# A transformer block on one Trainium2 core: the adapter's scores and softmax made beside the q projection, its products with the values from one compact 40-row tile

## The chip, the cores and the metric

The kernel runs on one core of a Trainium2 chip, as one program in one launch. Its time is the device time of one execution in microseconds (us); lower is better. The engines are PE (TensorE: matmuls, with PEld for its weight loads), DVE (VectorE), ACT (ScalarE), POOL (GpSimd) and SP (SyncE), which here only issues DMAs. PE writes to PSUM, eight banks of 128 x 512 f32; POOL neither reads nor writes it.

## The reference, cut to what matters

The attention of the block adds to the ordinary causal output, head by head, a second softmax over ten adapter tokens. Its scores use the rotated q of the same head, its scale is that of the whole width (C = 1024), and it has no mask:

```python
q = _apply_rope(q, cos, sin)                       # T = 2048, 32 heads of 32
...
_, ak, av = jnp.split(jnp.einsum('btc,oc->bto', adapter_wte[None], w_attn), 3, axis=-1)   # 10 tokens
ascores = jnp.einsum('bhqd,xhkd->bhqk', q, ak) / jnp.sqrt(jnp.asarray(C, x.dtype))
ascores = gating[0] * jax.nn.softmax(ascores, axis=-1)
y = y + jnp.einsum('bhqk,xhkd->bhqd', ascores, av)
```

Around it stand a modulated layernorm and the qkv projection (in front of it), and the output projection and a mixture of eight experts, two for each token (behind it).

## The kernel before

The program has three stages, and a barrier of all engines stands between them: `front`, `attention` and `tail`.

**front.** The normalized input lies in SBUF as hT_hi and hT_lo, two f32r parts of an f32 number, and each product is three matmuls (hi x hi, hi x lo, lo x hi). The loop over `n` makes 64 units, 32 of k and then 32 of q. A unit is one weight tile (128 columns, a group of four heads) times a quarter of the tokens (512): 8 steps k of 3 matmuls (L602 to L604) into one of two PSUM banks `acc[:, n % 2]`. Units go in halves of 16: four quarters times four weight tiles. DVE then rotates the unit (`rotate`: L406, L407, L409, L410) into `y[:, n % 2]`, ACT rounds it to y_hi (L264), POOL takes the rest y_lo in the place of y (`low_y`, L482), and SP stores both (`store`, L175). `rotate(n)` waits until the stores of unit n - 2 have landed. Between units PE also does parts of the modulation (`mod`, L523, from a 2 MB weight load into w_raw) and of the adapter's keys and values; POOL splits the next half's weights (L470, L472, L487). The 32 tiles of v (L625, L632) follow. The adapter's keys `ak` and values `av` end as tiles of 128 x 128 for each group of four heads, zero outside the four 32 x 32 blocks of a head with itself; in each block ten columns of ak, and ten rows of av, are used.

**attention.** Before its main loop stands a head of 16 turns (`TURNS`). A turn is one group of four heads times 1024 tokens: SP loads q_hi and q_lo (`load_pair`, L862, 512 KB each), POOL adds them (`a_add`, L1346), PE makes the scores with eight f32 matmuls of 40 columns (`a_score`, L1043), DVE takes the largest, subtracts, sums and inverts (L1290, L1294, L1299, L1301), ACT takes the exponential (L1152), POOL multiplies into `a_prob`, ten of every 32 columns (`a_spread`, L1353), PE transposes eight times (`a_turn_over`, L1053), ACT copies (L1158), PE multiplies av by it twice, 512 columns each and both in the one bank `y_acc` (`a_multiply`, L1062), ACT copies (L1164) and stores (L1169) to `scratch_a_y`, from where the main loop reads it back.

Spread over the turns by `head_share`, PE and DVE do the first 76 of the items with which the main loop later finds each row's largest score (`see`, L976 on PE, three banks `seen`; `largest`, L1237 or L1243 on DVE), which need the quarters of q and k that SP loads (`load_quarter`, L846). An item of PE waits until DVE has freed its bank. The main loop starts with L999, after a pair of L1095.

## Time and profile before

| | us |
|---|---|
| three timed runs | 2723.43, 2725.85, 2728.96 |
| their median | 2725.85 |
| profiled execution | 2727.61 |
| its span from the first instruction to the last | 2725.7 |
| its mean granted TensorE clock | 0.947 of full speed |

The profiled execution is 1.9 us longer than its span; what lies around the span is launch and end. It is 1.8 us longer than the median. In a row of a timeline stand the start, the time from the first to the last of what it merges, the engine and the line; behind it, in square brackets, the idle time before it with what ended it. Rows 2 are of the 32 units of q and of the head of the attention stage.

### The profile page before, as it was taken

The numbers are of one execution on the slowest core, as the hardware profiler recorded it, in microseconds if no ns is written. First come the engines' busy times: TensorE is split into PE (matmuls) and PEld (weight loads), VectorE is DVE, ScalarE is ACT, GpSimd is POOL, SyncE is SP. The second block draws the span as 40 slices with busy tenths as digits, with TensorE's granted clock in tenths as the row PEclk, the third lists the DMA queues.
The fourth block names the chain that finished last, engine by engine and source line by source line (L and its number), as shares of the span: only waits on it lengthen the run. The fifth ranks groups of instructions, "written<-read, shape, count | busy, mean of one in ns | idle before, by whom it ended". The sixth has DMA issues, their size and how long they took to land. (4 is left out here: it accounts for less than half of the span.)

```text
span 2725.7 us, 39161 instructions
## 1 busy us (share of the span) xinstructions
PE 2491.5 (91%) x13391; PEld 1630.1 (60%) x13391; DVE 1593.0 (58%) x3130; ACT 1051.3 (39%) x1860; POOL 1313.7 (48%) x824
## 2 busy tenths in 40 slices
PE   6789999999578999999999999998889876999997
PEld 4667676777454444444444444443368765888885
DVE  5544554210256777777777777777236554777665
ACT  3420011111135655555555555555601111444443
POOL 4351442100365766676766676765724452332332
PEclk8899999999589999999999999998989887999998
DMA  7356556311953524252515151513266745888885
GB/s 265 109 155 201 160 165 183 100 39 51 223 202 103 113 55 111 56 115 54 116 49 120 42 131 40 133 34 79 77 203 216 168 113 183 305 299 294 302 287 178
DMA packets 224849, 397.18 MB, mean 146 GB/s; under 512 B 43756, under 2 KB 94380, under 8 KB 224564
## 3 DMA queue, kind: packets, MB, share of 16 engines
q1 hardware_dynamic: 199588, 319.56, 40.9%
q0 software_dynamic: 17152, 50.38, 5.3%
q10 hardware_dynamic: 7952, 25.21, 2.9%
q8 instruction: 91, 1.49, 0.2%
q14 instruction: 66, 0.54, 0.1%
HBM read 299.16 MB, written 103.76 MB: 148 GB/s over the span
## 5 line engine op out<-in xcount | busy, mean ns | idle before, releaser
L1397 POOL TENSOR_TENSOR t_two<-t_prob 128x1024 f32<-128x1024 f32 (+1 forms) x321 | 688.2, 2164 | 181.1 <-ACT t_prob L1207 107.7
L1207 ACT ACTIVATE t_prob<-t_scores_psum 128x512 f32<-128x512 f32 (+3 forms) x1280 | 611.1, 537 | 387.8 <-PE t_scores_psum L999 194.9
L1237 DVE TENSOR_REDUCE t_part<-t_seen_psum 128x1 f32<-128x512 f32 x768 | 480.8, 681 | 165.3 <-PE t_seen_psum L976 161.0
L976 PE MATMUL t_seen_psum<-t_k_stack,t_q_stack 96*128 96x512 f32 (+3 forms) x1283 | 517.1, 412 | 24.2 <-DVE t_part L1237 15.8
L999 PE MATMUL t_scores_psum<-t_q_stack,t_k_stack 97*128 97x512 f32 (+3 forms) x1280 | 506.1, 407 | 5.9 <-ACT t_prob L1207 4.4
L999 PEld LDWEIGHTS t_scores_psum<-t_q_stack,t_k_stack 97*128 97x128 f32 x1280 | 244.0, 191 | 310.0 <-ACT t_prob L1207 172.4
L1243 DVE CUSTOM_DVE_ANT_0 t_seen_psum<-t_seen_psum,t_causal 128x128 f32<-128x128 f32 (+3 forms) x515 | 250.0, 504 | 106.3 <-PE t_seen_psum L976 96.1
L1019 PE MATMUL t_y_acc_psum<-t_prob,t_v 128*32 128x512 f32 (+3 forms) x2560 | 304.9, 549 | 0.0
L976 PEld LDWEIGHTS t_seen_psum<-t_k_stack,t_q_stack 96*128 96x128 f32 x1283 | 253.2, 199 | 67.1 <-DVE t_part L1237 30.7
L1678 PE MATMUL acc_psum<-z_e_hi,z_x_hi 128*128 128x512 f32 x576 | 228.3, 396 | 0.0
L1680 PE MATMUL acc_psum<-z_e_hi,z_x_lo 128*128 128x512 f32 x576 | 225.2, 391 | 0.0
L1679 PE MATMUL acc_psum<-z_e_lo,z_x_hi 128*128 128x512 f32 x576 | 224.7, 390 | 0.0
L602 PE MATMUL f_acc_psum<-hT_hi,f_w_hi 128*128 128x512 f32 x512 | 208.4, 407 | 2.0 <-POOL f_w_lo L472 1.7
L603 PE MATMUL f_acc_psum<-hT_lo,f_w_hi 128*128 128x512 f32 x512 | 202.8, 396 | 0.0
L604 PE MATMUL f_acc_psum<-hT_hi,f_w_lo 128*128 128x512 f32 x512 | 202.3, 395 | 0.0
L482 POOL TENSOR_TENSOR f_y<-f_y,f_y_hi 128x512 fp32r<-128x512 f32 x64 | 83.8, 1310 | 219.9 <-ACT f_y_hi L264 219.5
L264 ACT ACTIVATE f_y_hi<-f_y 128x512 fp32r<-128x512 f32 x64 | 40.4, 631 | 333.8 <-DVEq L411 333.7
L1032 PE MATMUL t_total_psum<-t_two,t_ones 128*32 128x512 f32 (+1 forms) x1296 | 160.7, 569 | 1.9 <-POOL t_two L1397 1.9
L1748 ACT ACTIVATE z_x_hi<-z_turned_psum 128x1024 fp32r<-128x1024 f32 x38 | 38.7, 1019 | 223.6 <-PE z_turned_psum L1664 223.6
L602 PEld LDWEIGHTS f_acc_psum<-hT_hi,f_w_hi 128*128 128x128 f32 x512 | 98.3, 192 | 40.4 <-issue 9.1
L1680 PEld LDWEIGHTS acc_psum<-z_e_hi,z_x_lo 128*128 128x128 f32 x576 | 108.5, 188 | 23.0
L1679 PEld LDWEIGHTS acc_psum<-z_e_lo,z_x_hi 128*128 128x128 f32 x576 | 108.7, 189 | 21.6
(240 smaller groups left out, 3804.1 us busy)
## 6 DMA issues: line engine op xcount, KB each, us to landing
z_raw<-in_expert_w SPq DMA_DIRECT2D x80, 512.0 KB, 5.3
z_spare<-in_expert_w SPq DMA_DIRECT2D x72, 512.0 KB
f_w_raw<-in_wmod SPq DMA_DIRECT2D x8, 2048.0 KB, 10.1
t_q_stack<-scratch_q_hi SPq DMA_DIRECT2D x64, 256.0 KB, 5.3
t_k_stack<-scratch_k_hi SPq DMA_DIRECT2D x64, 256.0 KB, 5.2
f_w_raw<-in_w_attn SPq DMA_DIRECT2D x24, 512.0 KB, 6.1
t_inverse<-scratch_inverse SPq DMA_DIRECT2D x132, 64.0 KB
t_y<-scratch_a_y SPq DMA_DIRECT2D x33, 256.0 KB
```

What stands on the lines that cost most here:

```text
L602: nc.tensor.matmul(acc[:, n % 2], lhs[0], rhs[0], start=(k == 0), stop=False)
L603: nc.tensor.matmul(acc[:, n % 2], lhs[0], rhs[1], start=False, stop=False)
L976: nc.tensor.matmul(seen[:, n % BANKS, 0:width], q_stack[par][0:STACK, h, t0:t0 + P], k_stack[par][0:STACK, h, c * CH:c * CH + width], star ...
L999: last = nc.tensor.matmul(scores[:, score_bank(step, h), c0:CH], k_stack[par][0:TOPS, h, kt * P:(kt + 1) * P], q_stack[par][0:TOPS, h, qc ...
L1019: last = nc.tensor.matmul(y_acc[h * D:(h + 1) * D, c0:CH], v[par][:, kt, h * D:(h + 1) * D], prob[:, step % RING, h, c0:CH], start=(kt == ...
L1207: nc.scalar.activation(prob[:, step % RING, h, c0:CH], scores[:, score_bank(step, h), c0:CH], ACT.Exp, scale=1.0 / math.sqrt(D)).then_inc( ...
L1237: nc.vector.tensor_reduce(dst, seen[:, n % BANKS], AX.X, ALU.max).then_inc(seen_free, 1)
L1243: nc.vector.tensor_tensor_reduce(out=at, in0=at, in1=causal[:, CH - width:CH], scale=1.0, scalar=MASKED, op0=ALU.add, op1=ALU.max, accum_o ...
L1397: nc.gpsimd.tensor_tensor(two[:, pair % 2, heads, c0:CH], a, b, ALU.add).then_inc(two_ready, 1)
L1678: nc.tensor.matmul(acc[:, s, col], x_hi[:, s, k], e_hi[:, k, col], start=(k == 0), stop=False)
L1679: nc.tensor.matmul(acc[:, s, col], x_hi[:, s, k], e_lo[:, k, col], start=False, stop=False)
L1680: last = nc.tensor.matmul(acc[:, s, col], x_lo[:, s, k], e_hi[:, k, col], start=False, stop=(k == KC - 1))
```

## The change

Scores and softmax leave the attention stage and are made in `front`, unit by unit, straight from the f32 tile `y[:, n % 2]` of a unit of q (`ask`, four matmuls; `lower`, `exponent`, `invert`, `spread`). They land in the PSUM banks `turned`, and in the second half of the tile av, which is not yet written then, and in the tile stats. The names `av`, `f_stats` and `f_turned` in the order's rows are these. SP stores 160 probabilities for each of 128 tokens of each unit to a new scratch in HBM (`store_prob`). The attention stage loads them with four DMAs (`load_prob`), and no q. Its 16 turns become 32 (`ASKS`) of 512 tokens: four transposes of 40 columns into 40 x 512, one ACT copy, and one matmul with `a_v`, a tile of 40 rows (ten for each head) that four DMAs gather from av into the tile `both`. Its product goes in turn to a bank of `scores` and to `y_acc`. POOL has in the head only the gating product and the memsets left. The items of `see` are the same, spread over the 32 turns on PE and in one row on DVE.

```diff
+        AM = TPC * HG
+        spare = av[:, G // 2:G, :].rearrange("p g n -> p (g n)")
+        weight = spare[:, 0:2 * AM * A].rearrange("p (b m a) -> p b m a", b=2, a=A)
+        prob = spare[:, 2 * AM * A:3 * AM * A].rearrange("p (m a) -> p m a", a=A)
...
+            def store_prob(m):
+                _, i, q, s = place(QUERIES + m)
+                t, x = (i * HG + s) * (NQ // 2) + q // 2, q % 2
+                sp.wait_ge(prob_ready, m + 1)
+                sp.dma_start(a_prob_d[t, :, x * AM * A:(x + 1) * AM * A], prob.rearrange("p m a -> p (m a)")).then_inc(prob_stored, 16)
...
+                if asked(n) >= 3:
+                    store_prob(asked(n) - 3)
...
+            def exponent(m):
+                act.wait_ge(shifted, m + 1)
+                at = weight[:, m % 2].rearrange("p m a -> p (m a)")
+                nc.scalar.activation(at, at, ACT.Exp, scale=1.0 / math.sqrt(C)).then_inc(exp_done, 1)
...
+            def lower(m):
+
+                dve.wait_ge(scored, m + 1)
+                if m > 0:
+                    dve.wait_ge(shifted, m)
+                view = turned[:, m % 2, 0:AM * A].rearrange("p (m a) -> p m a", a=A)
+                nc.vector.tensor_reduce(top, view, AX.X, ALU.max).then_inc(topped, 1)
+                dve.wait_ge(topped, m + 1)
+                if m >= 2:
+                    dve.wait_ge(prob_ready, m - 1)
+                nc.vector.tensor_tensor(weight[:, m % 2], view, top.rearrange("p (m a) -> p m a", a=1).broadcast_to([P, AM, A]),
+                                        ALU.subtract).then_inc(shifted, 1)
+
+            def invert(m):
+                dve.wait_ge(exp_done, m + 1)
+                if m > 0:
+                    dve.wait_ge(inv_ready, m)
+                nc.vector.tensor_reduce(total, weight[:, m % 2], AX.X, ALU.add).then_inc(summed, 1)
+                dve.wait_ge(summed, m + 1)
+                if m >= 1:
+                    dve.wait_ge(prob_ready, m)
+                nc.vector.reciprocal(inv, total).then_inc(inv_ready, 1)
...
+                if asked(n) >= 2:
+                    invert(asked(n) - 2)
+                if asked(n) >= 1:
+                    lower(asked(n) - 1)
+            invert(QUERIES - 2)
+            lower(QUERIES - 1)
+            invert(QUERIES - 1)
...
+                if asked(n) >= 0:
+                    pool.wait_ge(scored, asked(n) + 1)
...
+            def spread(m):
+                pool.wait_ge(inv_ready, m + 1)
+                if m >= 1:
+                    pool.wait_ge(prob_stored, 16 * m)
+                nc.gpsimd.tensor_tensor(prob, weight[:, m % 2], inv.rearrange("p (m a) -> p m a", a=1).broadcast_to([P, AM, A]),
+                                        ALU.mult).then_inc(prob_ready, 1)
...
+            def ask(m):
+
+                _, i, q, s = place(QUERIES + m)
+                n = QUERIES + m
+                pe.wait_ge(y_ready, n + 1)
+                if m == 0:
+                    pe.wait_ge(hi_done, NQ * KC)
+                    pe.wait_ge(second_taken, number_of["adapter_k", 1] - FIRST_EVENTS + 1)
+                if m >= 2:
+                    pe.wait_ge(shifted, m - 1)
+                for j in range(TPC):
+                    last = nc.tensor.matmul(turned[:, m % 2, j * HG * A:(j + 1) * HG * A], y[:, n % 2, j * P:(j + 1) * P],
+                                            ak[:, i * HG + s].rearrange("p (h a) -> p h a", a=D)[:, :, 0:A], start=True, stop=True)
+                last.then_inc(scored, 1)
...
+                    if k == ASK_AT and asked(n) >= 1:
+                        ask(asked(n) - 1)
...
+        a_v = both[0:HG * A].rearrange("p b n -> p (b n)").rearrange("p (g n) -> p g n", n=P)
+        a_turned_at = lambda u: scores[0:HG * A, u % 2]
+        a_acc = lambda u: scores[:, 2] if u % 2 == 0 else y_acc[:, :]
...
+            def load_prob(b):
+                at = slice(b * TURNS // 4, (b + 1) * TURNS // 4)
+                sp.dma_start(a_prob[:, at], a_prob_d[at].rearrange("t p n -> p t n")).then_inc(a_prob_loaded[b], 16)
+
+            sp.dma_start(ident[:, :], consts["ident"]).then_inc(consts_loaded, 16)
+            load_prob(0)
+            for h in range(HG):
+                sp.dma_start(a_v[h * A:(h + 1) * A, :, :], av[h * D:h * D + A, :, :]).then_inc(a_v_loaded, 16)
+            sp.dma_start(gating[:, :], consts["gating"].rearrange("(a n) -> a n", a=1).broadcast_to([P, 1])).then_inc(a_v_loaded, 16)
...
+            for dst, name in ((causal[:, :], "causal"), (after, "after")):
+                sp.dma_start(dst, consts[name]).then_inc(consts_loaded, 16)
...
+            def a_turn_over(u):
+
+                t, x = divmod(u, 2)
+                if t % (TURNS // 4) == 0:
+                    pe.wait_ge(a_prob_loaded[t // (TURNS // 4)], 16)
+                if u >= 2:
+                    pe.wait_ge(a_turn_ready, u - 1)
+                for j in range(TPC):
+                    cols = slice((x * TPC + j) * HG * A, (x * TPC + j + 1) * HG * A)
+                    last = nc.tensor.transpose(a_turned_at(u)[:, j * P:(j + 1) * P], a_prob[:, t, cols], ident[:, :])
...
+            pe.wait_ge(consts_loaded, 48)
+            for u in range(ASKS + 1):
+                if u < ASKS:
+                    a_turn_over(u)
+                head(u, 0)
+                if u >= 1:
+                    a_multiply(u - 1)
+                head(u, 1)
...
+            for n in range(HEAD):
+                advance(0, n)
...
+            pool.wait_ge(a_v_loaded, 80)
+            nc.gpsimd.tensor_scalar(a_v[:, :, :], a_v[:, :, :], gating[0:HG * A, 0:1], None, ALU.mult).then_inc(a_gated, 1)
+            pool.wait_ge(a_gated, 1)
+            for b in range(2):
                 nc.gpsimd.memset(k_stack[b][STACK:TOPS, :, :].bitcast(F32), 1.0).then_inc(one_rows_set, 1)
...
+                nc.tensor.matmul(a_acc(u), a_v[:, u // NQ], a_turn[:, u % 2], start=True, stop=True).then_inc(a_acc_ready, 1)
```

`asked(n)` is n - 32. `ask(asked(n) - 1)` stands inside unit n, after its step k = 5, and takes the tile of unit n - 1. On PE, in the front, this is a place inside a unit of q, before:

```order
L602 MATMUL f_acc_psum<-hT_hi,f_w_hi 128x512
L603 MATMUL f_acc_psum<-hT_lo,f_w_hi 128x512
L604 MATMUL f_acc_psum<-hT_hi,f_w_lo 128x512
L602 MATMUL f_acc_psum<-hT_hi,f_w_hi 128x512
L603 MATMUL f_acc_psum<-hT_lo,f_w_hi 128x512
```

and of the change:

```order
L697 MATMUL f_acc_psum<-hT_lo,f_w_hi 128x512
L698 MATMUL f_acc_psum<-hT_hi,f_w_lo 128x512
L680 MATMUL f_turned_psum<-ak,f_y 128x40 x4
L696 MATMUL f_acc_psum<-hT_hi,f_w_hi 128x512
L697 MATMUL f_acc_psum<-hT_lo,f_w_hi 128x512
```

The four matmuls of 40 columns stand among the 24 of the unit, with six of its matmuls behind them; nothing else of the unit moved. On PE, in the head of attention, one turn before (t_seen is an item's bank):

```order
L1053 MATMUL t_scores_psum<-t_ident,a_prob 128x128 x8
L1043 MATMUL t_scores_psum<-ak,a_q 128x40 x8
L976 MATMUL t_seen_psum<-t_k_stack,t_q_stack 128x384
L976 MATMUL t_seen_psum<-t_k_stack,t_q_stack 128x512
L1062 MATMUL t_y_acc_psum<-a_turn,av 128x512 x2
L976 MATMUL t_seen_psum<-t_k_stack,t_q_stack 128x128
L976 MATMUL t_seen_psum<-t_k_stack,t_q_stack 128x256
L1053 MATMUL t_scores_psum<-t_ident,a_prob 128x128 x8
L1043 MATMUL t_total_psum<-ak,a_q 128x40 x8
```

and two turns of the change:

```order
L1073 MATMUL t_seen_psum<-t_k_stack,t_q_stack 128x512 x2
L1142 MATMUL t_scores_psum<-t_ident,a_prob 40x128 x4
L1073 MATMUL t_seen_psum<-t_k_stack,t_q_stack 128x512
L1151 MATMUL t_scores_psum<-a_turn,t_both 128x512
L1073 MATMUL t_seen_psum<-t_k_stack,t_q_stack 128x512
L1142 MATMUL t_scores_psum<-t_ident,a_prob 40x128 x4
L1080 MATMUL t_seen_psum<-t_ident,t_top 16x128
L1151 MATMUL t_y_acc_psum<-a_turn,t_both 128x512
L1073 MATMUL t_seen_psum<-t_k_stack,t_q_stack 128x512
L1142 MATMUL t_scores_psum<-t_ident,a_prob 40x128 x4
```

The scores' matmuls (40 columns) are gone from here, the two products stand in different banks, and the items stand in smaller groups between them. On SP, at the start of the attention stage, before:

```order
L862 DMA a_q_hi<-scratch_q_hi 128x1024
L862 DMA a_q_lo<-scratch_q_lo 128x1024
L846 DMA t_q_stack<-scratch_q_hi 32x4x512
L846 DMA t_q_stack<-scratch_q_lo 32x4x512
L846 DMA t_q_stack<-scratch_q_hi 32x4x512
L846 DMA t_k_stack<-scratch_k_hi 32x4x512 x2
L846 DMA t_k_stack<-scratch_k_lo 32x4x512
L872 DMA t_ident<-in_ident 128x128
L872 DMA t_causal<-in_causal 128x512
L872 DMA t_y_own<-in_after 128x128
L872 DMA t_gating<-in_gating 128x1
L862 DMA a_q_hi<-scratch_q_hi 128x1024
```

and of the change (t_both is the tile of values):

```order
L957 DMA t_ident<-in_ident 128x128
L955 DMA a_prob<-scratch_a_prob 128x4x320
L960 DMA t_both<-av 10x1024 x4
L961 DMA t_gating<-in_gating 128x1
L938 DMA t_q_stack<-scratch_q_hi 32x4x512
L938 DMA t_q_stack<-scratch_q_lo 32x4x512
L938 DMA t_q_stack<-scratch_q_hi 32x4x512
L938 DMA t_k_stack<-scratch_k_hi 32x4x512 x2
L938 DMA t_k_stack<-scratch_k_lo 32x4x512
L964 DMA t_causal<-in_causal 128x512
L964 DMA t_y_own<-in_after 128x128
L938 DMA t_q_stack<-scratch_q_hi 32x4x512
```

The pair of q is gone; one load of probabilities, and four small ones inside SBUF, stand ahead of the first quarter of q and k.

## Rows read from the trace of the kernel before

**Rows 1.** The page: the span, and the busy time of each engine

```profile
span 2725.7 us, 39161 instructions
...
PE 2491.5 (91%) x13391; PEld 1630.1 (60%) x13391; DVE 1593.0 (58%) x3130; ACT 1051.3 (39%) x1860; POOL 1313.7 (48%) x824
```

**Rows 2.** Windows: length; busy PE, PEld, DVE, ACT, POOL; clock; DMA share; GB/s

```profile
285.70:490.10 204.40, 191.24 (x836) 142.64 (x834) 105.47 (x168) 24.26 (x36) 69.49 (x46) 0.97 0.58 170
...
682.50:851.20 168.70, 118.30 (x543) 82.97 (x543) 70.78 (x179) 43.52 (x65) 78.80 (x39) 0.77 0.68 195
```

**Rows 3.** Timeline, the start of the attention stage

```profile
682.53 0.35 SPq L862 DMA_DIRECT2D a_q_hi<-scratch_q_hi  x1
...
699.18 0.23 DVE L1230 CAST t_ident_b<-t_ident 128x128 bf16<-128x128 f32 x1 [15.84 <-DMA t_gating<-in_gating]
```

**Rows 4.** Groups of instructions, window 682.5 to 851.2

```profile
L1346 POOL TENSOR_TENSOR a_q<-a_q_hi,a_q_lo 128x1024 f32<-128x1024 f32 x16 | 37.6, 2350 | 154.4 <-DMA a_q_lo<-scratch_q_lo 154.4
...
L1237 DVE TENSOR_REDUCE t_part<-t_seen_psum 128x1 f32<-128x512 f32 x44 | 28.0, 682 | 9.2 <-PE t_seen_psum L976 8.9
...
L1164 ACT ACTIVATE a_y<-t_y_acc_psum 128x512 f32<-128x512 f32 x32 | 19.0, 593 | 31.5 <-PE t_y_acc_psum L1062 31.5
...
L1158 ACT ACTIVATE a_turn<-t_scores_psum 128x1024 f32<-128x1024 f32 x16 | 16.4, 1024 | 19.6 <-PE t_scores_psum L1053 19.6
...
L1243 DVE CUSTOM_DVE_ANT_0 t_seen_psum<-t_seen_psum,t_causal 128x128 f32<-128x128 f32 (+3 forms) x32 | 15.0, 510 | 6.6 <-PE t_seen_psum L976 6.6
...
L1353 POOL TENSOR_TENSOR a_prob<-a_weight,a_inv 128x320 f32<-128x320 f32 x16 | 11.8, 737 | 25.7 <-DVE a_inv L1301 25.6
...
L1299 DVE TENSOR_REDUCE a_total<-a_weight 128x32 f32<-128x320 f32 x16 | 7.6, 476 | 0.0
```

**Rows 5.** Timeline of PE, late turns of the head

```profile
809.65 3.63 PE L1043 MATMUL t_scores_psum<-ak,a_q 128*128 128x40 f32 x16 [5.31 <-POOL a_q L1346]
...
816.77 1.10 PE L1062 MATMUL t_y_acc_psum<-a_turn,av 128*128 128x512 f32 x2 [0.78 <-ACT a_y L1164]
...
819.28 1.88 PE L1043 MATMUL t_total_psum<-ak,a_q 128*128 128x40 f32 x16
820.99 0.71 PE L976 MATMUL t_seen_psum<-t_k_stack,t_q_stack 96*128 96x512 f32 x2
821.54 1.02 PE L1062 MATMUL t_y_acc_psum<-a_turn,av 128*128 128x512 f32 x2
823.42 1.10 PE L1062 MATMUL t_y_acc_psum<-a_turn,av 128*128 128x512 f32 x2 [0.86 <-ACT a_y L1164]
823.95 1.26 PE L976 MATMUL t_seen_psum<-t_k_stack,t_q_stack 96*128 96x512 f32 x3
...
827.62 0.70 PE L976 MATMUL t_seen_psum<-t_k_stack,t_q_stack 96*128 96x512 f32 x2
...
847.54 1.10 PE L1062 MATMUL t_y_acc_psum<-a_turn,av 128*128 128x512 f32 x2 [0.78 <-ACT a_y L1164]
...
851.18 0.50 PE L999 MATMUL t_scores_psum<-t_q_stack,t_k_stack 97*128 97x512 f32 x1
```

**Rows 6.** Timeline, one ordinary unit of q, from 450.65

```profile
450.65 0.39 PE L602 MATMUL f_acc_psum<-hT_hi,f_w_hi 128*128 128x512 f32 x1
...
453.17 0.69 DVE L410 TENSOR_TENSOR f_y<-f_y,f_x_rot 128x512 f32<-128x512 f32 x1
...
456.09 0.39 PE L602 MATMUL f_acc_psum<-hT_hi,f_w_hi 128*128 128x512 f32 x1
```

**Rows 7.** Timeline of PE, start of a half's modulation work

```profile
308.85 3.64 PE L523 MATMUL f_small_psum<-f_w_raw,f_silu_rep 128*32 128x512 f32 x16 [5.31 <-DMA f_w_raw<-in_wmod]
```

**Rows 8.** Timeline, a rotation beside a weight split of POOL

```profile
474.16 2.39 POOL L487 TENSOR_TENSOR f_w_lo<-f_w_raw,f_w_hi 128x1024 fp32r<-128x1024 f32 x1 [1.89 <-ACT f_w_hi L271]
...
474.29 2.81 DVE L409 TENSOR_TENSOR f_x_rot<-f_x_rot,f_cos_sin 128x512 f32<-128x512 f32 x1 [0.15 <-DVE f_y L407]
```

**Rows 9.** DMA issues: KB each, median us from issue to landing

```profile
scratch_v<-f_y_hi SPq DMA_DIRECT2D x32, 256.0 KB, 2.3
```

More of the change, by code:

```diff
@@ L220, in _ @@
                         load_w(5, slot)
+                if 1 <= m <= 3:
+                    store_prob(QUERIES - 4 + m)
                 store_v(m)
@@ L507, in _ @@
                 low_y(n)
+                if asked(n) >= 3:
+                    spread(asked(n) - 3)
                 if u > HALF_UNITS - HG and half < 3:
@@ L511, in _ @@
                     split_w((half + 2) * HG - 1)
+            for m in range(QUERIES - 3, QUERIES):
+                spread(m)
             even_w(5 * HG, 4 * HG + 3)
@@ L647, in _ @@
                         lead(m + 1)
+                    else:
+                        ask(QUERIES - 1)
                     pe.wait_ge(w_ready, 4 * HG + 2 * hv + 2)
@@ L697, in attention @@
             ab("filler", [P, 2 * HG * T])
-            a_y, a_turn = ab("y", [P, 2, 2 * CH]), ab("turn", [P, 2, 2 * CH])
-            a_prob, a_weight = ab("prob", [P, 2, 2 * CH]), ab("weight", [P, 2, AM, A])
-            a_top, a_total, a_inv = ab("top", [P, AM]), ab("total", [P, AM]), ab("inv", [P, 2, AM])
-            a_q, a_parts = ab("q", [P, 2, 2 * CH]), [ab(f"q_{n}", [P, 2, 2 * CH]) for n in ("hi", "lo")]
+            a_prob, a_y = ab("prob", [P, TURNS, 2 * TPC * HG * A]), ab("y", [P, 2, 2 * CH])
+            a_turn = ab("turn", [HG * A, 2, CH])
         q_stack, k_stack = [None, None], [None, None]
@@ L1034, in add_up @@
                 last.then_inc(total_done, 1)
-            def a_score(t):
-                g = a_group(t)[0]
-                pe.wait_ge(a_q_ready, t + 1)
-                if t >= 2:
-                    pe.wait_ge(a_shifted, t - 1)
-                for j in range(2 * TPC):
-                    last = nc.tensor.matmul(a_scores(t)[:, j * HG * A:(j + 1) * HG * A], a_q[:, t % 2, j * P:(j + 1) * P],
-                                            ak[:, g].rearrange("p (h a) -> p h a", a=D)[:, :, 0:A], start=True, stop=True)
-                last.then_inc(a_scores_ready, 1)
@@ L1047, in a_turn_over @@
-            def a_turn_over(t):
-                pe.wait_ge(a_prob_ready, t + 1)
-                if t >= 1:
-                    pe.wait_ge(a_turn_ready, t)
-                for j in range(2 * TPC):
-                    last = nc.tensor.transpose(a_turned_at[:, j * P:(j + 1) * P], a_prob[:, t % 2, j * P:(j + 1) * P], ident[:, :])
+            def a_turn_over(u):
[7 more added lines that the diff above has]
+                    last = nc.tensor.transpose(a_turned_at(u)[:, j * P:(j + 1) * P], a_prob[:, t, cols], ident[:, :])
@@ L1065, in head @@
-            def head(t, half):
-                for n in head_share(t, half):
+                if u >= 2:
+                    pe.wait_ge(a_y_ready, u - 1)
+                nc.tensor.matmul(a_acc(u), a_v[:, u // NQ], a_turn[:, u % 2], start=True, stop=True).then_inc(a_acc_ready, 1)
+            def head(u, half):
+                for n in head_share(u, half):
                     if order[n][0] == "see" and order[n][3:] == (0, 0, 0):
@@ L1190, in take_total @@
                 act.wait_ge(tall_loaded, (i * W + wi + 2) * 16)
[L1191 removed]
+                nc.scalar.activation(whole, total[:, :], ACT.Copy).then_inc(total_free, 1)
             def finish(i, step):
```

220 lines of the change are left out of this document (74 added, 146 removed).

## The prediction

> **What bounds the kernel now.** I read the page first: PE is busy for 91% of the span, the others for 58% or less [rows 1]. Then two windows, for the share is not even. In the 32 units of q PE is busy for 191.2 of 204.4 us at a clock of 0.97, DVE for 105.5: more work for PE makes these units longer. In the head of the attention stage PE is busy for 118.3 of 168.7 us, at a clock of 0.77 [rows 2]. The groups of that window say why: POOL waited for the second part of a q pair, 154.4 us in 8 waits (the first began in the stage before; POOL is busy for 78.8 of 168.7 us, so at most 89.9 fall in here), and its add of 2.35 us stands before each turn's scores [rows 2, 4]. Late in the head, where the clock is full, a turn takes 6.63 us (820.99 to 827.62) [rows 5]. So the change takes work from a stretch that waits and puts some of it into a stretch that PE fills. Everything from L999 on is the same program.
>
> **The units of q: what is added on PE.** A unit has 24 matmuls in 5.44 us (450.65 to 456.09) [rows 6]. Eight score matmuls take 1.71 us at the full clock, from 819.28 to the next row at 820.99 [rows 5]; four take 0.85, and 32 times that is 27.4 us. Some of it is covered: at the start of each half of q PE idles for a 2 MB weight load (5.31 us, and a second place like it) [rows 7], and that load is issued behind POOL's splits, which the change leaves in place. The three scorings ahead of the first wait and four ahead of the second, 7 x 0.85 = 6.0 us, fit in. Left: 21.4 us.
>
> **The units of q: waits that are added.** `ask(n)` stands 18 matmuls, 18 x 0.227 = 4.1 us, into unit n + 1, and the last step of the rotation ends 3.21 us into it (453.17 + 0.69 against 450.65, the first row of the unit behind the one rotated) [rows 6]: 0.9 us to spare. Behind the waiting matmuls stand six more of the unit; POOL's `low_y` waits for the scores too, so the stores leave about 1.5 us later in a unit, and `rotate` waits for them two units on, which are now 1.7 us longer: no loss. New work on DVE is two reductions, a subtraction and a reciprocal over half the elements of L1299's 476 ns [rows 4]: by my estimate four at 0.25 to 0.35, with gaps some 1.6 us, on top of 3 of rotation in a unit of 6.3. It fits, as do ACT's exponential and POOL's product (737 ns for double the elements). Where POOL splits weights it doesn't fit: L409, 0.69 us elsewhere, took 2.81 beside L487's 2.39 [rows 8]. The rotation then ends near 5.3 us, and `ask` waits 1.2. I count four such places, and 2 us more where v begins (ACT's exponential stands before the last weight rounding, and `ask(31)` waits for the last rotation): 7 us. The units and the change to v grow by 28 us. Bounds: 21 if no wait is new; 42 if every third unit waits 2 us too.
>
> By the Trainium skill ("SBUF — State Buffer", Who interferes with whom) a VectorE instruction with two SBUF inputs and a GpSimd one that reads SBUF exclude each other for a whole instruction. The trace agrees: L409 ended 0.55 us after the split [rows 8]. By that rule all seven splits beside q units would hold a rotation, not four, which gives 3.6 us more; it stays inside the bounds.
>
> **The head: its start.** The first load is issued at 682.53 and the constants have landed at 699.18, 16.7 us later, behind 12 DMAs of 3.0 MB [rows 3]. PE now waits for them before anything else, behind 15 DMAs of 2.8 MB (64 KB, 655 KB of probabilities, 0.16 MB of av, the quarter's 1.6 MB, 0.3 MB). I keep 16.7. PE has then idled for over 20 us. After a wait of 5.31 us the scores took 3.63 us instead of 1.88, and 7.1 us passed (809.65 to 816.77) before a product took 1.10 again [rows 5]: half speed for 7 us costs 3.5.
>
> **The head: its turns.** Of the 6.63 us the scores' 1.71 go. The two products share a bank: the second starts 1.88 us after the first (821.54, 823.42), while a product alone keeps PE 0.53 (823.42 to 823.95) [rows 5]; with two banks 1.35 go. Transposes of 40 columns and products of 40 rows are taken at their old price. Left are 3.57 us for a turn, 57.1 for 16. The others are close to that: DVE needs 28.0 + 15.0 for its two kinds of item and a few us to read accumulators, some 47; ACT 19.0 + 16.4 and 16 issues of stores, some 41 [rows 4]. Three engines that wait for each other, two of them with 82 and 72% of PE's work, cost something: I take 61. The end, from the last product to L999, was 3.64 (847.54 to 851.18) [rows 5] and stays. Sum: 16.7 + 3.5 + 61 + 3.6 = 84.8, against 168.65 (682.53 to 851.18): 83.9 less. Bounds: 16.7 + 57.1 + 3.6 = 77.4 (nothing lost at the start or by coupling) and 16.7 + 7 + 16 x 4.92 + 3.6 = 106 (only the scores go from a turn). What POOL keeps, memsets and the gating product, is 78.8 - 37.6 - 11.8 = 29.4 us [rows 2, 4]. It begins early and lies beside PE's turns; without that cover it would end at most those 29.4 after the start, which is still inside the 84.8.
>
> **The sum.** 2727.6 + 28 - 83.9 = 2671.7 for an execution like the profiled one, which is 1.8 above the median of the runs: 2670. The bounds together give 2727.6 + 21 - 91.3 = 2657 and 2727.6 + 42 - 62.7 = 2707.
>
> **The rivals.**
> - Transfers set the head. It moved 195 GB/s for 168.7 us, 32.9 MB [rows 2]. Without 16.8 MB of q and with 2.6 MB of probabilities it is 18.7. At the same rate that is 96 us, not 84.8. For it: the quarters, v and the stores of a_y now fall in half the time, and a product's copy waits for the store two turns back. Against it: the loads no longer wait for turns, so most are issued in the first 35 us. 2727.6 + 28 - 72.7 = 2683; 0.15.
> - The front's loop gets longer than PE's work: rotation, scores, `low_y`, store, and the rotation two units on form a circle in which scores are new. If 1.5 us of it can't be hidden in each unit, 48 us come on top: 2718. Against it is the sum above; for it, that a weight split already moves a rotation's end by 2.1 us [rows 8], and nothing in the circle is buffered more than twice. 0.07.
> - Slower than before. There is one buffer `prob`: `spread(m)` waits until `store_prob(m - 1)` has landed, and the next unit's `low_y`, its stores and the 2 MB loads are queued behind it on POOL and SP. The circle is 0.4 of product, some 0.7 of issue and waits, and the landing. With the 2.3 us of a v store [rows 9] it is 3.4 of 6.3 and hidden. It eats the whole gain of 56 when it reaches 6.3 + 56/32 = 8.05, a landing of 7 us for each of these stores of 640 bytes a row; with 9 us the time is 2727.6 + 28 - 83.9 + 32 x 3.8 = 2793. 0.04.
> - The gain isn't there: L999 waits for something not named here (the last quarter, v, a memset) and the head stays over 140 us: 2727. 0.03.
>
> **How the numbers follow.** The forecast has 0.71, with 2655 to 2700 as its own range. The first rival lies in it, the second partly outside. I give 2653 to 2705, which leaves out the last two, most of the second, and a little on each side. A measurement of this kernel tells 0.2% (5.5 us) from no change. Faster: forecast, first and second rival, 0.93. Same: 0.03. Slower: 0.04.
>
> **What would show it.** A unit of q of 6.3 us, the row after four 40-column matmuls 0.85 behind their start; waits of PE for the rotation's last step at four places or so; a first transpose 16 to 17 us after the stage's first DMA; turns of 1.8 to 2.0 us of 512 tokens; the main loop's first matmul some 85 us behind that DMA. Wrong would be: PE waiting in most q units; ACT waiting for stores of a_y; a start of over 25 us behind the small loads of av; the clock staying at half in the head.

## The result, and the profile after

| | before | after |
|---|---|---|
| median of six timed runs, us | 2724.22 (2715.87 to 2728.96) | 2744.52 (2739.88 to 2750.76) |
| ratio of the two, 95% interval | | 1.0081 (1.0058 to 1.0103) |
| profiled execution, us | 2727.61 | 2750.76 |
| its span, us | 2725.7 | 2748.9 |
| its mean granted TensorE clock | 0.947 | 0.934 |

The changed kernel is 0.8% slower. Forecast were 2670 us and "faster". The ratios below leave out one execution of `swap`, an experiment, that took 5961.5 us.

The first row of [rows 2] begins at 285.70, where the second unit of q begins, so it holds 31 of the 32; with the first it is

```profile
280.26:490.10 209.84, 196.68 (x860) 147.15 (x858) 110.40 (x172) 24.26 (x36) 74.50 (x49) 0.97 0.57 168
```

Where the time went is read from the rows at which the stages begin and end, in the two profiled executions:

| stretch, us | before | after | difference | forecast |
|---|---|---|---|---|
| first unit of q to first matmul of v | 209.84 | 245.55 | +35.7 | +28 with the next row |
| v, to the first DMA of attention | 192.43 | 194.51 | +2.1 | |
| head, to the first matmul of the main loop | 168.65 | 152.43 | -16.2 | -83.9 |
| main loop | 1116.35 | 1116.02 | -0.3 | 0 |
| the rest behind it | 758.17 | 760.77 | +2.6 | 0 |

So the front costs 10 us more than forecast, and the head gives 68 us less. The page of after shows little of this: PE is busy for one point more of the span than before [rows 1], and the other engines are within one point of what they were.

```profile
span 2748.9 us, 39393 instructions
...
PE 2539.2 (92%) x13391; PEld 1632.9 (59%) x13391; DVE 1599.3 (58%) x3194; ACT 1059.0 (39%) x1893; POOL 1295.2 (47%) x823
```

The windows of the changed kernel show it: here the q units, the wait at the start of the head, and the head from its first transpose on, then four pieces of it and the start of the main loop (length; busy PE, PEld, DVE, ACT, POOL; clock; DMA share; GB/s).

```profile
279.62:525.17 245.55, 231.58 (x1108) 176.96 (x1106) 136.08 (x290) 35.38 (x67) 85.43 (x77) 0.96 0.53 155
719.68:738.15 18.47, 0.00 (x0) 0.00 (x0) 0.10 (x2) 1.28 (x1) 11.53 (x3) 0.50 0.82 174
738.15:872.11 133.96, 132.29 (x287) 55.93 (x287) 52.94 (x114) 38.02 (x64) 16.83 (x4) 0.50 0.40 118
...
740.00:760.00 20.00, 19.02 (x44) 8.54 (x42) 10.11 (x29) 5.94 (x10) 14.98 (x4) 0.50 0.97 233
780.00:800.00 20.00, 20.00 (x43) 8.59 (x42) 7.58 (x16) 5.70 (x11) 0.00 (x0) 0.50 0.58 176
820.00:840.00 20.00, 20.00 (x43) 8.30 (x42) 8.03 (x13) 5.50 (x10) 0.00 (x0) 0.50 0.20 79
840.00:860.00 20.00, 20.00 (x42) 8.46 (x42) 8.11 (x12) 5.78 (x10) 0.00 (x0) 0.50 0.13 53
...
872.00:876.00 4.00, 4.00 (x25) 2.38 (x21) 2.65 (x6) 2.85 (x6) 0.00 (x0) 0.89 0.00 0
876.00:900.00 24.00, 23.45 (x155) 11.81 (x154) 18.66 (x51) 15.30 (x35) 15.44 (x11) 1.00 0.34 80
```

The reader is to look at two numbers of one row: PE is busy for 132.29 of 133.96 us, and its clock is 0.50, that is 1.2 GHz of 2.4, throughout. It is hardly ever idle and gets the full clock only when the main loop has begun. The kernel before did the opposite: with more idle time its clock was 0.77 over the head [rows 2], and in two pieces of it:

```profile
780.00:800.00 20.00, 17.48 (x107) 13.20 (x107) 12.69 (x38) 7.84 (x12) 11.16 (x6) 1.00 0.36 143
...
820.00:840.00 20.00, 16.77 (x94) 11.92 (x93) 14.45 (x28) 7.82 (x13) 6.04 (x5) 1.00 0.26 106
```

PE's timeline of the changed head, one turn of 1024 tokens (an x2 in a product's row is one f32 matmul in its two records):

```profile
781.94 2.07 PE L1151 MATMUL t_scores_psum<-a_turn,t_both 40*128 40x512 f32 x2
783.95 0.79 PE L1073 MATMUL t_seen_psum<-t_k_stack,t_q_stack 96*128 96x512 f32 x1
784.54 1.05 PE L1142 MATMUL t_scores_psum<-t_ident,a_prob 128*40 128x128 f32 x4
785.24 0.78 PE L1073 MATMUL t_seen_psum<-t_k_stack,t_q_stack 96*128 96x512 f32 x1
785.95 2.07 PE L1151 MATMUL t_y_acc_psum<-a_turn,t_both 40*128 40x512 f32 x2
...
789.96 1.22 PE L1151 MATMUL t_scores_psum<-a_turn,t_both 40*128 40x512 f32 x1
```

Nothing stands in brackets, so PE waits for nobody: 4.0 us for 512 tokens where 1.8 to 2.0 was forecast. `40*128` is the part of the array that a matmul uses: a product now uses 40 of 128 rows, a transpose 40 of 128 columns. The products of the head before used 128 of 128 [rows 5].

The waits of the q units in the changed kernel (engine, what waited, what ended it: us in total, times, longest):

```profile
POOL f_y L550 <- PE f_turned_psum L680: 150.5, 29, 7.3
ACT av L308 <- DVE av L459: 107.7, 29, 5.0
...
DVE f_stats L470 <- POOL av L556: 83.3, 28, 3.9
PEld f_turned_psum L680 <- DVEq L447: 20.2, 19, 2.8
PE f_turned_psum L680 <- DVEq L447: 11.0, 10, 2.4
```

PE waits for the end of a rotation (L447) in ten places, its weight loads (PEld) in nineteen, and DVE, which has to rotate, waits 83.3 us for POOL's `spread` (L556). The timeline of one unit without any extra work shows the order of it:

```profile
475.14 1.29 POOL L550 TENSOR_TENSOR f_y<-f_y,f_y_hi 128x512 fp32r<-128x512 f32 x1 [5.17 <-PE f_turned_psum L680]
476.30 0.39 PE L696 MATMUL f_acc_psum<-hT_hi,f_w_hi 128*128 128x512 f32 x1
...
476.38 0.47 POOL L556 TENSOR_TENSOR av<-av,f_stats 128x160 f32<-128x160 f32 x1
...
476.95 0.25 DVE L470 RECIPROCAL f_stats<-f_stats 128x16 f32<-128x16 f32 x1 [2.61 <-POOL av L556]
...
477.68 0.74 DVE L442 STREAM_SHUFFLE f_x_rot<-f_acc_psum 128x512 f32<-128x512 f32 x1
...
480.67 1.08 PE L680 MATMUL f_turned_psum<-ak,f_y 128*128 128x40 f32 x8
...
481.90 1.30 POOL L550 TENSOR_TENSOR f_y<-f_y,f_y_hi 128x512 fp32r<-128x512 f32 x1 [5.05 <-PE f_turned_psum L680]
```

`low_y` (L550) waits for the scores of `ask`, which stand in PE's next unit. `spread` stands behind it on POOL. The one buffer `inv` lets `invert` (L470) write only when `spread` of the unit before has read it. `lower` and the rotation (L442) stand behind `invert` on DVE, and the next `ask` waits for that rotation. The rotation now starts 1.38 us into a unit (477.68 against 476.30), and `ask` runs 4.37 us into it. This unit takes 6.75 us (476.30 to 483.05), not 6.3. PE's own row shows no wait in it; what waits is the weight load of the scores, 0.55 us ahead of 480.67.

### The profile page after: what moved, and what is told of

The parts are those of the page before. It is cut to its first block and busy times, and to the rows that moved or that the text cites. A ratio compares the mean times of both kernels' runs of the same rounds, so it can differ in the third digit from the quotient of the medians.

```text
span 2748.9 us, 39393 instructions
## 1 busy us (share of the span) xinstructions
PE 2539.2 (92%) x13391; PEld 1632.9 (59%) x13391; DVE 1599.3 (58%) x3194; ACT 1059.0 (39%) x1893; POOL 1295.2 (47%) x823
## 5 line engine op out<-in xcount | busy, mean ns | idle before, releaser
L1073 PE MATMUL t_seen_psum<-t_k_stack,t_q_stack 96*128 96x512 f32 (+3 forms) x1283 | 534.4, 422 | 19.4 <-DVE t_part L1314 15.1
L1073 PEld LDWEIGHTS t_seen_psum<-t_k_stack,t_q_stack 96*128 96x128 f32 x1283 | 260.4, 204 | 99.0 <-issue 39.1
L696 PE MATMUL f_acc_psum<-hT_hi,f_w_hi 128*128 128x512 f32 x512 | 211.7, 414 | 0.0
L550 POOL TENSOR_TENSOR f_y<-f_y,f_y_hi 128x512 fp32r<-128x512 f32 x64 | 83.2, 1299 | 242.3 <-PE f_turned_psum L680 159.0
L1412 POOL MEMSET t_prob<- 128x512 f32 x64 | 33.6, 525 | 214.7 <-PE t_total_psum L1129 182.5
L1923 DVE SCALAR_TENSOR_TENSOR z_x_in<-acc_psum,z_ids_a,z_gb 128x1024 f32<-128x1024 f32 x36 | 46.1, 1279 | 143.6 <-DMA z_ids_a<-scratch_table 143.6
```

What stands on the lines that cost most here:

```text
L696: nc.tensor.matmul(acc[:, n % 2], lhs[0], rhs[0], start=(k == 0), stop=False)
L1073: nc.tensor.matmul(seen[:, n % BANKS, 0:width], q_stack[par][0:STACK, h, t0:t0 + P], k_stack[par][0:STACK, h, c * CH:c * CH + width], star ...
```

## The experiments

The stage times below are of the profiled execution of each kernel; the ratios are to the kernel before, timed on the same chip. Seven kernels have the front as it was changed (the change itself, rows128, cols128, both128, warm, dense, thin): their stretch from the first unit of q to v took 243.5 to 248.7 us, 246.1 on the mean, so a difference of under 5 us in it says little from one profile. Single units of q (between every eighth of the L696 rows) repeat far better, within 0.05 us for two thirds of them.

**The head: the clock.** Two causes were open: narrow operations (theory 1), or the idle start (theory 2).

`rows128`: the product over 128 rows, those behind the 40th zero.

```diff
-            a_turn = ab("turn", [HG * A, 2, CH])
+            a_turn = ab("turn", [P, 2, CH])
...
-        a_v = both[0:HG * A].rearrange("p b n -> p (b n)").rearrange("p (g n) -> p g n", n=P)
+        a_v = both[:, :].rearrange("p b n -> p (b n)").rearrange("p (g n) -> p g n", n=P)
...
+            nc.gpsimd.memset(both[:, :, :], 0.0).then_inc(a_cleared, 1)
+            nc.gpsimd.memset(a_turn[:, :, :], 0.0).then_inc(a_cleared, 1)
```

> The head of attention with the product of each turn made over 128 rows instead of 40 (rows 40 to 127 of the values are zero, so the result is the same); the same instructions, columns and order. In the changed kernel every window of the head showed a granted clock of 0.50 while PE was busy for all of it, and the head lasted 152.4 us. Theory 1: the clock that is granted depends on how much of the array the work uses, and products of 40 rows use too little. Then it rises in the head, and the head comes to 85 to 110 us: 2744.5 minus 42 to 65, so 2680 to 2702. Theory 2: the clock is low only because the stage starts from an idle stretch of over 20 us, and nothing in its steady flow ever makes it rise. Then this stays at 0.50 and 2744, within 3.

`cols128`: transposes with 128 columns of the loaded tile.

```diff
-                    cols = slice((x * TPC + j) * HG * A, (x * TPC + j + 1) * HG * A)
-                    last = nc.tensor.transpose(a_turned_at(u)[:, j * P:(j + 1) * P], a_prob[:, t, cols], ident[:, :])
+                    at = (u * TPC + j) * HG * A
+                    width = min(P, TURNS * 2 * TPC * HG * A - at)
+                    last = nc.tensor.transpose(a_turned_at(u)[0:width, j * P:(j + 1) * P], a_wide[:, at:at + width], ident[:, :])
```

> The same with the other small operation: the transposes of the probabilities take 128 columns of the loaded tile instead of 40 (the extra ones are the neighbouring probabilities; only the first 40 rows are copied on). Products stay at 40 rows. Theory 1 (use of the array): transposes are four short instructions of 128 columns beside a product of 512 columns at four passes, so they are the smaller share of the work, and the clock rises less than in rows128, if at all: 2700 to 2744. Theory 2 (start from idle): 2744, within 3.

`both128` is both, and also copies all 128 transposed rows, so that the product's moving rows 40 to 127 hold neighbouring probabilities and only its values are zero there.

> Both edits together: transposes of 128 columns, all 128 rows copied, product over 128 rows (values zero behind row 40). Theory 1: the clock is full for most of the head, which comes to 85 to 95 us: 2680 to 2690. Theory 2: 0.50 and 2744 as before, within 3.

`warm` gives PE wide work while it waits at the start.

```diff
+            for _ in range(20):
+                nc.tensor.matmul(total[:, :], av[:, 4], av[:, 0:4].rearrange("p g n -> p (g n)"), start=True, stop=True)
             pe.wait_ge(consts_loaded, 48)
```

> The changed kernel with 20 extra matmuls of 128 rows and 512 columns on PE, into a bank that is not yet used, where PE waits for the constants at the start of the attention stage; nothing else. Theory 2 (the clock is low only since the stage starts from idle): with PE kept busy until the first transpose the clock starts full and stays full, the head is 85 to 95 us and the time 2680 to 2690. Theory 1 (small operations do not hold the clock): it starts full, falls back to 0.50 within some 10 us of the small operations, and the time is 2738 to 2746.

| | time, us | ratio (95%) | head, us | clock over the head |
|---|---|---|---|---|
| the change | 2744.5 | 1.0081 (1.0058 to 1.0103) | 152.4 | 0.50 |
| rows128 | 2679.8 | 0.9841 (0.9819 to 0.9863) | 96.3 | 0.79 |
| cols128 | 2739.0 | 1.0045 (1.0022 to 1.0069) | 152.6 | 0.50 |
| both128 | 2678.2 | 0.9841 (0.9804 to 0.9879) | 92.1 | 0.83 |
| warm | 2739.4 | 1.0066 (1.0044 to 1.0087) | 152.4 | 0.57 (0.52 from 740 on) |

The windows of rows128 (the first) and of warm (the second), cut at the first transpose or thereabouts:

```profile
719.17:737.69 18.52, 0.00 (x1) 0.01 (x1) 0.11 (x2) 1.28 (x1) 13.16 (x5) 0.50 0.80 173
737.69:815.42 77.73, 68.42 (x287) 40.56 (x287) 52.14 (x114) 37.09 (x64) 17.06 (x4) 0.85 0.67 202
```

```profile
721.16:740.00 18.84, 18.80 (x41) 8.27 (x42) 0.78 (x3) 1.28 (x1) 11.89 (x3) 0.92 0.80 179
740.00:873.59 133.59, 130.13 (x287) 54.98 (x285) 52.60 (x114) 38.00 (x64) 16.46 (x4) 0.52 0.40 117
```

Theory 2 falls twice. rows128 starts from the same idle stretch and its clock rises by itself, 8.9 us behind the first transpose; warm has 0.92 over its start and is at half from 744.9 on, 5 us into the kernel's own work. Theory 1 holds in its main point: the same 287 matmuls with the same columns keep PE busy for 68.4 us instead of 132.3 once a product uses 128 rows. The rows added in rows128 hold zeros on both sides and were enough. Transposes of 128 columns do nothing by themselves; beside wide products their worth can't be told (92.1 against 96.3 us here, 96.8 against 95.6 in the pair below).

**Is it the narrow product as such?** `dense` adds one matmul over 128 rows behind each product, `thin` the same over 40 rows (`[0:40]` for `[0:128]`).

```diff
                     a_multiply(u - 1)
+                    nc.tensor.matmul(total[:, :], av[0:128, 4], av[0:128, 0:4].rearrange("p g n -> p (g n)"), start=True, stop=True)
```

> The changed kernel with one extra matmul behind each of the 32 products of the head, 128 rows by 128 columns against 512, into a bank that nothing else uses there. Everything of the kernel itself keeps its 40 rows. It asks whether the clock stays low because of the narrow products as such, or because too little of the array is in use over all. Theory 1 (use of the array over all): the added wide work makes the clock rise as in rows128, so that PE does more and is done sooner; steady units of 512 tokens take 1.8 + 0.9 = 2.7 us instead of 3.9 to 4.4, the head 110 to 125 us instead of 152.4, the time 2700 to 2715. Rival (a narrow product in the flow keeps the clock low whatever stands beside it): it stays at 0.50, the units take 5.8, the head 205 to 215, the time 2795 to 2805.

> The same extra matmul, but over 40 rows; the control for dense: same count, columns and place. Both theories: the clock stays at 0.50, a unit takes 3.9 + 1.75 = 5.7 us, the head 205 to 212 us, the time 2790 to 2802. It also gives the price of a product over 40 rows at this clock: the growth of the head over 32, expected 1.7 to 1.9 us. If instead the head is under 160 us, PE was not the bound of the head and the extra work was hidden.

`dense` took 2705.2 us, ratio 0.9941 (0.9915 to 0.9967), `thin` 2788.0, ratio 1.0266 (1.0238 to 1.0294). Their heads, dense first, thin second:

```profile
724.43:850.43 126.00, 107.89 (x351) 49.46 (x351) 52.45 (x115) 39.27 (x65) 28.36 (x6) 0.85 0.53 151
```

```profile
716.91:923.06 206.15, 186.76 (x350) 77.30 (x350) 52.16 (x115) 39.27 (x65) 28.35 (x6) 0.50 0.34 92
```

With 32 useless wide matmuls the head is 26 us shorter than without them; with 32 useless narrow ones, 54 us longer. A narrow product in the flow does not by itself keep the clock low: matmuls over 128 rows beside it bring the clock up, the same number over 40 rows do not. dense's head is 1 us over the range that was given, thin's time 2 us under its own. thin also prices a product: (206.15 - 152.43) / 32 = 1.68 us at half the clock, and so by estimate 0.84 at the full one.

**The front: the circle.** `swap` exchanges two steps on POOL.

```diff
-                low_y(n)
                 if asked(n) >= 3:
                     spread(asked(n) - 3)
+                low_y(n)
```

> The changed kernel with two POOL steps of the loop over q units in the other order: spread of three units ago first, then low_y of this unit. Same instructions, same buffers. Theory F1 (a circle over the single inv buffer): low_y(n) now waits for the scores of ask(n), which stand in PE's unit n + 1; spread stands behind it, the reciprocal of invert waits for spread, lower and the next rotation wait behind the reciprocal, and the next ask waits for the rotation. With spread ahead of low_y the circle is open: an ordinary unit of q takes 6.3 us instead of 6.5 to 6.8, the last one (11.8) some 7.5, and the stretch from unit 32 to the first matmul of v 231 to 235 us instead of 245.6. Time 2731 to 2736. Theory F2 (DVE has too much of its own to do in a unit): units stay at 6.5 to 6.8 and the stretch within 2 us of 245.6.

It took 2721.4 us, ratio 1.0003 (0.9983 to 1.0022): as fast as the kernel before, with the head still at half the clock. The stretch to v is 235.90 us (0.9 over the range of F1), the ordinary unit 6.36, the last one 9.08: F1, with a last unit worse than expected. The rows of one ordinary unit in swap:

```profile
465.37 0.39 PE L696 MATMUL f_acc_psum<-hT_hi,f_w_hi 128*128 128x512 f32 x1
...
469.45 0.98 PE L680 MATMUL f_turned_psum<-ak,f_y 128*128 128x40 f32 x8
...
471.73 0.39 PE L696 MATMUL f_acc_psum<-hT_hi,f_w_hi 128*128 128x512 f32 x1
```

and the weight load's wait for the rotation, which was 20.2 us in 19 waits:

```profile
PEld f_turned_psum L680 <- DVEq L447: 11.9, 9, 1.9
```

Its profile is 31 us shorter than that of the change, of which 9.7 are in this stretch; its main loop was 11.6 us shorter too and what follows it 9.4, which the edit doesn't touch, and kernels with one main loop show 1102 to 1116 us for it. So the stretch gives the size, not the 23 us between the medians. Four kernels have this front (swap, rows_swap, both_swap and y3): 233.6 to 235.9 us, 234.6 on the mean, 11.5 below the mean of the seven. Single units show it more sharply: the 26th to the 29th unit of q, ordinary ones, take 6.75 to 6.90 us each in the seven kernels and 6.36 in the four. Not all of the 11.5 is the circle: the mean clock over the stretch was 0.96 to 0.98 in the seven and 0.98 to 1.00 in the four, and by the share of the low clock up to 5 us of the difference may be that (an estimate). Whether the waits brought the clock down was not tested.

`one_score` leaves out three of the four score matmuls in swap (`range(1)` for `range(TPC)` in `ask`).

> swap with one score matmul a unit instead of four (three quarters of the probabilities are made of what stood in the bank before, so its output is not the reference's). It sizes the term of the score matmuls: three of them, 0.64 us, are gone from each of 32 units. If PE's work sets the units, the stretch from unit 32 to v is 16 to 20 us shorter than in swap. If a wait sets them, it is less than 8 us shorter, and PE's waits for the last step of a rotation grow by the difference.

One execution, 2713.0 us. The stretch is 223.23 us, 12.7 less than in swap, between what the two readings gave. PE's waits for the rotation tell the rest:

```profile
PE f_turned_psum L680 <- DVEq L447: 15.8, 12, 3.2
```

In swap the same row is 8.2 us in 8 waits. 12.7 us are gained and 7.6 more are waited, together 20.3, and 32 x 3 matmuls of 0.21 us are 20.2. In ordinary units the work sets the time (5.71 us against 6.36); where POOL splits weights the rotation does.

**Both together.** `rows_swap` is rows128 with swap, `both_swap` both128 with swap.

> rows128 (2679.8 us) and swap together, for both stages at once. If the two faults are what they seem and independent, the gains add: F1 gives 2679.8 minus 10 to 14, so 2666 to 2670, ratio to the kernel before 0.978 to 0.981. F2 gives 2679, ratio 0.984.

> both128 (2678.2 us) and swap together. F1 gives 2664 to 2668, F2 2678. In its head the granted clock should be 0.95 or more from some 20 us behind the first transpose on, as in both128; if the transposes matter beside the product, its main loop starts 2 to 4 us earlier behind the stage's first DMA than that of rows_swap.

2671.2 us, ratio 0.9799 (0.9781 to 0.9818), and 2669.3 us, ratio 0.9800 (0.9774 to 0.9826), both some 1 us over the ranges given. The stretches to v are 233.6 us in both, the heads 95.6 and 96.8, so each stage keeps its gain beside the other. In the timed runs swap took 0.0042 off the ratio of rows128, but 0.0078 off that of the change; this difference was not followed up. both_swap's head was to be the shorter by 2 to 4 us and isn't. Such heads differ by their clock too: in both_swap it fell back to half once, for 6.8 us, in rows_swap twice, in both128 (head 92.1) never.

```profile
767.60:774.20 6.60, 3.85 (x10) 2.72 (x11) 0.69 (x3) 3.37 (x6) 0.00 (x0) 0.50 0.26 105
```

ACT's waits in both_swap's head say what is left:

```profile
ACT a_turn L1240 <- PE t_scores_psum L1146: 27.5, 16, 18.3
ACT a_y L1247 <- DMA scratch_a_y<-a_y: 13.2, 3, 6.1
```

In the changed kernel no such wait exists; there ACT waits for PE alone.

**What stands behind the clock.** `y3` is both_swap with a third buffer for the product's output (a_turn moves to other tiles for it).

```diff
-            a_prob, a_y = ab("prob", [P, TURNS, 2 * TPC * HG * A]), ab("y", [P, 2, 2 * CH])
+            a_prob, a_y = ab("prob", [P, TURNS, 2 * TPC * HG * A]), ab("y", [P, 3, 2 * CH])
...
-                if t >= 2:
-                    act.wait_ge(a_stored[t % 2], 16 * (t // 2))
+                if t >= 3:
+                    act.wait_ge(a_stored[t % 3], 16 * (t // 3))
```

> both_swap with three buffers for the output of the head's products instead of two. In both_swap, at the full clock, ACT waits 13.2 us in 3 waits (the longest 6.1) for stores of a_y, and its head lasts 96.8 us. Theory H1: that wait, hidden while the clock was half, is the next bound of the head; with a third buffer it shrinks to under 4 us, the head is 85 to 90 us, and the time 7 to 11 us shorter than both_swap's 2669: 2658 to 2662. Theory H2: the transfers of the head are at their limit, a third buffer only puts the wait off by a turn, and the head gets under 4 us shorter.

`y3_prob3` also divides in place, in three buffers of weights.

```diff
-        weight = spare[:, 0:2 * AM * A].rearrange("p (b m a) -> p b m a", b=2, a=A)
-        prob = spare[:, 2 * AM * A:3 * AM * A].rearrange("p (m a) -> p m a", a=A)
+        weight = spare[:, 0:3 * AM * A].rearrange("p (b m a) -> p b m a", b=3, a=A)
...
-                if m >= 1:
-                    pool.wait_ge(prob_stored, 16 * m)
-                nc.gpsimd.tensor_tensor(prob, weight[:, m % 2], inv.rearrange("p (m a) -> p m a", a=1).broadcast_to([P, AM, A]),
+                nc.gpsimd.tensor_tensor(weight[:, m % 3], weight[:, m % 3], inv.rearrange("p (m a) -> p m a", a=1).broadcast_to([P, AM, A]),
```

> y3, and in the front the probabilities are divided in place in three buffers of weights, so that spread no longer waits for the store before it. In both_swap POOL waits 100.1 us in 22 waits for that store in the stretch of the q units, and low_y stands behind it, while PE waits 10.2 us in 10 waits for rotations. Theory G1 (the store's landing reaches PE by way of low_y, its stores and the rotation two units on): the stretch from unit 32 to v, 233.6 us in both_swap, is 3 to 8 us shorter, and the time 2651 to 2658. Theory G2 (it is hidden; PE's waits come from DVE beside the weight splits): POOL's waits for the store go to nought and the stretch stays within 1.5 us, the time that of y3.

y3: 2672.8 us, ratio 0.9795 (0.9768 to 0.9821). y3_prob3: 2663.1 us, ratio 0.9767 (0.9738 to 0.9796), the lowest here, though the intervals of the three before it overlap its own. In the profile of y3 ACT's wait for stores falls to 6.3 us in 4 waits (H1 said under 4), and the head up to its first transpose and behind it is

```profile
710.20:728.93 18.73, 0.00 (x0) 0.00 (x0) 0.10 (x2) 1.28 (x1) 12.48 (x4) 0.50 0.81 177
728.93:796.08 67.15, 63.70 (x286) 40.79 (x286) 51.76 (x114) 36.95 (x64) 16.85 (x4) 0.93 0.78 232
```

so the head is 85.9 us (86.2 in y3_prob3), within the 85 to 90 of H1, 11 less than in both_swap and 6 less than in both128. Part of the 11 is the clock, which fell a second time in both_swap and not in y3. both128 and y3_prob3 had the low clock nearly equally long behind their first transpose and the full one from there on (both128 above):

```profile
739.78:751.80 12.02, 10.50 (x30) 7.01 (x31) 9.49 (x17) 3.59 (x6) 11.96 (x2) 0.50 1.09 232
751.90:813.44 61.54, 54.64 (x259) 34.65 (x257) 42.48 (x98) 33.20 (x58) 5.11 (x3) 1.00 0.62 209
```

```profile
724.74:737.20 12.46, 10.85 (x31) 7.30 (x31) 9.82 (x18) 3.59 (x6) 12.40 (x2) 0.50 1.08 223
737.40:792.58 55.18, 53.79 (x257) 34.45 (x256) 42.33 (x96) 33.86 (x58) 4.65 (x2) 1.00 0.69 233
```

Between these two the third buffer is worth 5.9 us, 92.1 against 86.2. The timed runs don't show it: the ratios of y3 and both_swap are the same within their intervals, so the 7 to 11 us that were expected are missing there.

In y3_prob3 POOL's waits for the store, 100.1 us in both_swap, are gone. The stretch to v is 232.0 us, against 233.6 in both_swap and 235.1 in y3, which fits neither G1 (3 to 8 less than both_swap) nor quite G2 (within 1.5). The units show where the store was felt: the 15th and 16th of q take 7.2 to 7.6 and 7.8 us in the four kernels with that wait, and 6.4 and 7.5 here, 1.1 to 1.5 us together. So nearly all of the 100 us had been hidden. By the medians y3_prob3 is 9.7 us faster than y3 on the same chip, more than the stretch explains; of the 7.3 us between the two profiles 3.5 lie behind the attention stage, which the edit doesn't touch. Why the rest is there stays open.

## Why the prediction was wrong, point by point

- **The head's clock: the step that failed.** "Half speed for 7 us costs 3.5" was taken from one place of the head of before, where the product's duration came back after a wait [rows 5]. It carried over that PE, once busy, gets its full clock. That held in heads with products over 128 rows, where the clock came back 4 to 13 us behind the first transpose (and in some fell once or twice more, for 6.8 us each). The change made every product one over 40 rows, and in its head the clock did not come back for 134 us; "taken at their old price" held only at the full clock. Price: the head takes 152.4 us against 92.1 to 96.3, 56 to 60 us; against y3, which has a third buffer too, 66.5. The forecast named this as what would make it wrong and gave it no chance among the rivals. The shape stands in every PE row, beside the clock of the windows, but no row of before showed narrow work alone, so it could have been a rival with a price, not more.
- By the Trainium skill (TensorE: Matmul & The Clock Gate, "What's actually happening") the gate looks at how busy PE has been, and activity releases it. The trace agrees where the products are over 128 rows (0.85 in rows128), and differs where they are over 40: PE was busy for 132.29 of 133.96 us at 0.50. The measurement decides: here a busy PE kept the lower clock.
- **The turns.** At the full clock the total was right: rows128 has 1.77 and 1.99 us for 512 tokens in the rows below, 1.77 on the mean of 23 such steps at the full clock, so 3.54 for a turn; forecast 3.57.

```profile
799.50 1.02 PE L1152 MATMUL t_scores_psum<-a_turn,t_both 128*128 128x512 f32 x2
799.96 0.79 PE L1074 MATMUL t_seen_psum<-t_k_stack,t_q_stack 96*128 96x512 f32 x1
...
801.27 1.02 PE L1152 MATMUL t_y_acc_psum<-a_turn,t_both 128*128 128x512 f32 x2
...
803.26 1.02 PE L1152 MATMUL t_scores_psum<-a_turn,t_both 128*128 128x512 f32 x2
```
   A part inside was wrong: a product read as 0.53 us costs 0.84 by the estimate from thin, since what was read is when the next record starts. The 1.35 us for two banks (1.88 - 0.53) rested on it and would be 1.04, the turn 3.88. So it is partly luck that 3.57 came out; which other part was off the other way isn't known.
- **The start** was forecast at 16.7 us and is 18.5 (719.68 to 738.15); the end 3.6, in rows128 3.1 (behind the last product's start).
- **Transfers in the head**, a rival with 0.15, are half right once the clock is full. It gave a head of 96 us; those with wide products and two buffers take 92.1 to 96.8. One reason it named is there: a product's copy waits for the store two turns back, 13.2 us of ACT's waits in both_swap, and a third buffer is worth 5.9 us. Its limit of 195 GB/s is not: behind its first 12 us y3_prob3 moved 233. With the third buffer, which the changed kernel doesn't have, the head is 85.9 us; 84.8 was forecast.
- **The units of q.** The score matmuls cost what was said: 0.65 us less for three of them (6.36 to 5.71), so 0.87 for four, forecast 0.85. The unit without waits is 6.36, forecast 6.3. The stretch without the circle, 232.0 to 235.9 us, is 22 to 26 above that of before; with the 2 us at v it is what was forecast, 28, with bounds of 21 and 42. Two terms in it were off against each other: in swap all 10.3 us of waits for the two weight loads are gone, where 6.0 were counted, and PE waits for rotations in eight places for 8.2 us, where four and 4.8 were.
- **The circle: the second step that failed.** "The stores leave about 1.5 us later in a unit ... no loss" followed `low_y` to SP and stopped there. `spread` stands behind it on the same engine, and `invert`, `lower` and the rotation behind `spread`. Asking of each instruction behind the delayed one who waits for it would have found it. Price: up to 11.5 us (swap and the others with its order), a part of which may be the clock. The rival with a circle named other members (rotation, store, rotation two units on) and put 48 us on it.
- **The single buffer `prob`**, the rival that was to end slower, costs little: of 100 us of waits some 1.5 reached PE. The kernel did end slower, but not by this way.
- **The sum** with what the runs show: the front +24.7 without the circle (234.6 against 209.8), +11.5 for it, +2 at v, together +38 as in the profiled pair; the head -83 in y3 (85.9 against 168.65), and 66.5 of it not had in the change, 56 to 60 by the clock and the rest by a wait that shows only at the full clock, together -16. With the small difference in the rest that is the +23 of the two spans. Mended, the kernel is at 0.9767, 2663 us. That it lies near the 2670 of the forecast doesn't confirm it: this kernel has wide products, another order on POOL, a third buffer for the products' output and the probabilities divided in place.

What stays open: how many rows would have been enough; that was not varied. Of few columns the runs say less: the main loop, with over 2500 matmuls on 32 of 128 columns among wider ones, had 0.98 before and after. Nor was it tried to fill the 40 columns of the transposes with useful ones, or to shorten the 18.5 us at the start.

## What to carry to other kernels

A change that narrows the matmuls of a stretch (here products from 128 rows to 40) can cost the clock of everything beside them, so "PE is busy for 100%" is read together with the granted clock and with the shapes in PE's rows, and padding with zeros is tried first. A wait that a change adds is followed through everything queued behind it on its engine, until it comes back to where it began or ends; the cure can be to exchange two lines.

## What the runs showed of the hardware

- PE busy for 132 of 134 us stayed at a granted clock of 0.50 with products over 40 rows and transposes of 40 columns; the same instructions with 128 rows in the products had 0.85 from the same start. Rows of zeros were enough for it.
- Work that is added can make the program shorter: 32 matmuls over 128 rows took the head from 152.4 to 126.0 us (clock 0.85). The same over 40 rows took it to 206.2 (0.50).
- The idle start isn't what kept the clock low: with 20 wide matmuls in it (0.92) the clock went back to half under the narrow work.
- The time from the start of a product's record to the next record is not what the product costs: the timeline shows 0.46 us in rows128 (799.50 to 799.96), while 32 added products cost 1.68 us each at half the clock (thin), an estimated 0.84 at the full one.
